# Products of probabilities with V issued in pairs of key tiles, in the attention of a one-core hybrid block

## What is computed

```python
q1, q2, k1, k2, v1, v2 = ...                     # 16 heads, D = 16, rotary on q and k
s = einsum('bthd,bshd->bhts', q, k) * scale      # causal mask
a = softmax(s)                                   # over the keys s
attn1 = concat(a1 @ v1, a1 @ v2); attn2 = concat(a2 @ v1, a2 @ v2)
attn = lowpass_over_tokens(attn1 - lambda_full * attn2)   # an FFT filter in the reference
attn = attn * rsqrt(mean(attn**2) + eps) * rms_weight * (1 - lambda_init)
x = x + attn.reshape(...) @ Wout
```

## Time and profile before

| | us |
|---|---|
| median of 3 runs | 1439.36 |
| lowest, highest | 1429.5, 1444.77 |
| the profiled execution | 1432.0 |
| its span in the trace | 1430.2 |
| TensorE busy in it | 1188.8 (83%) |
| VectorE, GpSimd, ScalarE busy | 892.3, 819.8, 602.6 |
| mean granted TensorE clock | 0.926 of full speed |

### The profile page before, as it was taken

One profiled execution on the slowest core, in us unless ns is written; L12 is line 12 of the kernel. 1 busy time (PEld: TensorE's weight loads), 2 busy tenths in 40 slices (PEclk: granted clock), 3 DMA queues, 4 the chain that ended last, 5 costly groups with the idle time before them and its releaser, 6 DMA issues. The chain is left out here.

```text
span 1430.2 us, 20085 instructions
## 1 busy us (share of the span) xinstructions
PE 1188.8 (83%) x7129; PEld 604.1 (42%) x7144; DVE 892.3 (62%) x1418; ACT 602.6 (42%) x969; POOL 819.8 (57%) x603
## 2 busy tenths in 40 slices
PE   5964888898898898898898888984679899986995
PEld 4721233333333433332332432422368777764443
DVE  5643756666666766665665775652666666663775
ACT  2310355565565555555555655662322232221121
POOL 4409457587687678678678674671025556663111
PEclk9987799899899999899999998986789999998997
DMA  4343220401401410410410310030422111113330
GB/s 146 114 135 97 74 77 12 118 23 38 118 30 31 119 40 21 119 43 18 119 42 18 104 56 5 1 133 0 166 87 74 59 64 70 45 45 103 125 103 38
DMA packets 72561, 101.20 MB, mean 71 GB/s; under 512 B 12432, under 2 KB 37904, under 8 KB 72464
## 3 DMA queue, kind: packets, MB, share of 16 engines
q1 hardware_dynamic: 61968, 70.57, 17.2%
q0 software_dynamic: 5888, 20.97, 3.8%
q10 hardware_dynamic: 4608, 8.39, 1.5%
HBM read 66.34 MB, written 33.55 MB: 70 GB/s over the span
## 5 line engine op out<-in xcount | busy, mean ns | idle before, releaser
L917 DVE TENSOR_REDUCE nm<-score 128x1 f32<-128x640 f32 (+6 forms) x352 | 348.8, 1024 | 275.6 <-PE score L802 210.3
L1127 POOL TENSOR_TENSOR base<-base,plain 128x2048 f32<-128x2048 f32 x48 | 218.7, 4556 | 79.0 <-ACT plain L1067 77.3
L1067 ACT ACTIVATE plain<-score 128x1024 f32<-128x1024 f32 (+3 forms) x288 | 208.1, 734 | 114.2 <-PE score L818 82.1
L813 PE MATMUL score<-qst,kst 98*128 98x512 bf16 (+7 forms) x768 | 201.2, 348 | 51.9 <-ACT plain L1067 28.2
L876 DVE TENSOR_TENSOR base<-base,plain 128x1536 f32<-128x1536 f32 (+2 forms) x96 | 165.1, 1720 | 15.5 <-ACT plain L1067 11.5
L712 PE MATMUL misc<-xnT,wg 128*128 128x512 f32 x256 | 128.6, 631 | 26.4 <-ACT raw L988 14.1
L1067 ACT ACTIVATE base<-score 128x1024 f32<-128x1024 f32 x96 | 98.1, 1024 | 86.8 <-PE score L818 45.8
L813 PEld LDWEIGHTS score<-qst,kst 98*128 98x128 bf16 (+1 forms) x768 | 57.1, 100 | 180.4 <-issue 67.7
L831 PE MATMUL acc<-plain,vg 128*32 128x512 f32 (+3 forms) x1152 | 116.8, 479 | 5.4 <-ACT plain L1067 4.9
L797 PE MATMUL score<-kst,qst 48*128 48x512 bf16 (+3 forms) x512 | 71.5, 358 | 46.7 <-DVE nm L917 26.9
L1431 PE MATMUL m_b<-m_winh,m_hTh 128*128 128x512 f32 x192 | 83.5, 435 | 13.9 <-DVE m_k L1610 12.5
(11 more groups left out here) (230 smaller groups left out, 2370.4 us busy)
## 6 DMA issues: line engine op xcount, KB each, us to landing
piece_scratch<-pieces POOLq DMA_DIRECT2D x16, 768.0 KB, 4.0
qst<-piece_scratch SPq DMA_DIRECT2D x192, 64.0 KB, 3.0
kst<-piece_scratch SPq DMA_DIRECT2D x192, 64.0 KB, 2.2
x1in<-in_query SPq DMA_DIRECT2D x16, 256.0 KB, 2.7
v_scratch<-v ACTq DMA_DIRECT2D x16, 256.0 KB, 2.0
vg<-v_scratch SPq DMA_DIRECT2D x8, 512.0 KB, 4.1
att_scratch<-y SPq DMA_DIRECT2D x8, 512.0 KB, 3.0
m_aT<-att_scratch SPq DMA_DIRECT2D x16, 256.0 KB, 2.9
```

Of the source, the lines that this page charges most:

```text
L813: mm = nc.tensor.matmul(score[k % RING][:, x, t0:HALF], kst[c, n % SLOTS, first + x, j * P:(j + 1) * P], qst[c, n % SLOTS, first + x, h * ...
L917: nc.vector.tensor_reduce(out, src, AX.X, ALU.max, negate=True).then_inc(s_max, 1)
L1067: nc.scalar.activation(tile_of(n, v)[:, first:first + 2, t0:HALF], score[k % RING][:, :, t0:HALF], ACT.Exp)\
L1127: nc.gpsimd.tensor_tensor(total, total, tile_of(n, v)[:, :, t0:HALF], ALU.add)\
```

## The change

The product of an even tile is no longer put behind its own probs steps, but directly ahead of the product of the odd tile that follows. Nothing else in the list moves.

```diff
@@ -408,6 +408,7 @@
 ROWS_OVER = 25
+PAIRED = 1
 ROOT_LATER, NEWTON_LATER = 3, 3
@@ -466,7 +467,11 @@
         for v in range(NV):
             k = at["probs", n, 2 * v + 1] + VALUES_LATER
-            put(k, ("values", n, v))
+            if not PAIRED:
+                put(k, ("values", n, v))
+            elif v % 2:
+                put(k, ("values", n, v - 1))
+                put(k, ("values", n, v))
             if v in ADDED:
                 put(k + ADD_LATER[ADDED[v][1]], ("add", n, v))
```

## The result

| | before | after |
|---|---|---|
| median, us | 1434.8 (4 runs, 1429.5 to 1444.77) | 1465.93 (4 runs, 1457.15 to 1466.34) |
| ratio | | 1.0215, interval 1.0177 to 1.0253 |
| profiled execution, us | 1432.0 | 1465.85 |
| its span, us | 1430.2 | 1464.0 |
| mean granted clock of TensorE in it | 0.926 | 0.912 |

The changed kernel is slower by 2.15%: 31 us between the medians, 34 between the two profiled executions. Forecast were 17 over 1439.4. The medians of before that came with the later runs (25, 28 and 7 of them) are 1433.75, 1432.79 and 1433.34. So the 1439.4 shown ahead was a few us high, and the 31 us are the better number.

What follows compares the result with a forecast made beforehand. TensorE, 83% busy, looked like the bound, with GpSimd nearly a second one in even sets (0.65 us to spare). Delays of +15.8 and clock +6 on 1432 gave 1454; forecast median 1456, 1.2% over 1439.4, range 1437 to 1468.

Steps and rivals of the forecast that it cites:

- The sum: Whole execution: +15.8 us of delays and +6 of clock over the profiled 1432, giving 1454; median forecast 1456.
- Add 5 waits for V4: GpSimd, even sets: add 5 overwrites tile 4, which the moved product V4 reads, so it starts 2.85 us late.
- Absorption by the gap before add 6: GpSimd, even sets: of 0.88 us idle before add 6, 0.7 absorbs delay; 2.15 us stays, making `shp` late.
- TensorE comes earlier to the turn, at 635.0: TensorE reaches its turning of `shp` 1.2 us earlier, then waits 2.8 us for GpSimd; the turn is 1.6 late.
- 2.5 us go through to each pair: Behind the turn of `shp`: 2.5 us late passes to the next pair of sets; five pairs, +12.5 us.
- the clock, "Seven new waits by 4/7 by 1.6 makes +6.4": New waits before the turn of `shp` lower TensorE's clock in some sets; bounds 0 and 11 us, +6 taken.
- n = 12 and 13, and n = 14 with the end: Late sets: +1.5 us for n = 12 and 13, +1.0 for n = 14, add 5 of the last set 1.3 late.
- the sets 0 and 1: First two sets, without a Newton step, keep some of the pairs' saving: -0.5 us.
- Only the drains count: Rival: TensorE is the bound and GpSimd isn't late; faster, median 1432 or so, 1425 with all drains; chance 0.09.
- No difference: Rival: short wait at the turn of `shp`, clock stays up; +6 to +12 us, 1445 to 1451; chance 0.29.
- Slower by more: Rival: each new wait lowers the clock and the odd set's long idle grows; +28 us, 1467; chance 0.12.
- About 13 us less of TensorE's busy time (in spite of the clock): Sign expected in the profile after: TensorE busy about 13 us less, with paired products 0.89 us apart.

Runs made afterwards that it cites:

- run 10: Kernel before with no product moved, only add 5 on GpSimd made to wait for V5 instead of V4; 1455.87 us, ratio 1.0147 to before.
- run 4: Changed kernel, all six pairs kept, with the second Newton step of a set six steps later, behind `shp`; 1436.04 us, ratio 1.0015 to before.
- run 2: Kernel before with only V4 and V5 (products with V of tiles 4 and 5) made a pair; 1464.22 us, ratio 1.018 to before.
- run 1: Changed kernel with V4 back at its old place and the other five pairs kept; 1440.09 us, ratio 1.006 to before.
- run 6: Changed kernel with V4 at its old place and the second Newton step of a set six steps later; 1445.47 us, ratio 1.0075 to before.
- run 8: Kernel before with pairs of the other parity, V1-V2, V5-V6 and V9-V10, the other products alone; 1447.28 us, ratio 1.0084 to before.
- run 3: Kernel before with only V0 and V1 made a pair; 1429.17 us, ratio 0.995 to before.

## Why the prediction was right, and where its sizes were off

Right in sign, in mechanism and within the range, too low by 14 of the 31 us. The sum itself was +22 on the profiled execution, where 33.9 were measured; the +17 of the median was a choice, over a median of before that was some 5 us high.

- **Add 5 waits for V4.** Forecast 2.85 late, measured 3.36: V4 began 13.56 us behind the anchor at 605.50 instead of 13.24, and add 5 1.24 us behind it instead of 1.05. The idle is ended by `acc` and no longer by ScalarE, as forecast. Run 10, in which add 5 waits for V5 at its old place, shows this one step to be worth 22 of the 31 us.
- **Absorption by the gap before add 6.** Forecast 0.7, leaving 2.15; measured 0.71 (0.88 - 0.17), and 2.64 left, the same half us too much as above.
- **TensorE comes earlier to the turn, at 635.0.** It didn't: 43.46 us behind the anchor instead of 43.51. The two products of a pair are 0.15 us cheaper each, near the forecast, but the -1.2 for V0's place and the pairs doesn't arrive at the turn. Between the anchor and the turn the rows have 2.05 us of idle time in six pieces, against 1.60 in three before, so small waits took up 0.45 of it; where the rest went isn't shown. So the wait was 2.19 instead of 2.8, and with it the turn was 2.14 late, not 1.6.
- **2.5 us go through to each pair.** Measured +2.6, +2.5 and +2.6 in n = 2, 6, 10, the three pairs without a fall of the clock behind the turn. The number is right, by two errors that cancel: the turn was 0.5 us later than forecast, and what was added behind it is 0.4 (2.5 less 2.14) instead of the 0.9 for V0.
- **The term that failed: the clock, "Seven new waits by 4/7 by 1.6 makes +6.4".** The count was right: it fell behind four of the seven. But the 4/7 was taken from other waits, and behind the turns of runs 2 and 10, with 1.5 and 1.8 us, it fell in none of n = 2 to 10, so that the count came out was luck. The price was wrong. It was taken from a fall of 3.4 us, seen from the next engine as 1.6 us. Measured are 6.8 us at 1.2 GHz behind the turn, and more later in the same pair: the pairs n = 4 and 8 cost 8.0 and 6.9, so 5.5 and 4.4 us above the 2.5. In the whole attention the time at 1.2 GHz went from 103 to 150 us. At half speed that is some 23 us of work's time; some of it lies in waits that were there anyway.
- **n = 12 and 13, and n = 14 with the end.** Forecast +1.5 and +2.3. Measured by the windows: 56.2 + 45.4 against 48.9 + 46.4 us, +6.3, and 74.2 against 69.0, +5.2. The turns of these sets waited 2.73 and 2.38 us (for n = 14 I had counted on 1.1 us of slack) and both brought the clock down. The windows of before, and V11 of the last set now, which starts at 1003.53 against 969.65:

```profile
805.30:854.20 48.90, 43.55 (x334) 18.40 (x336) 31.87 (x33) 28.44 (x40) 32.41 (x19) 0.97 0.18 54
854.20:900.60 46.40, 39.17 (x300) 13.92 (x300) 29.65 (x31) 25.71 (x35) 21.49 (x11) 0.89 0.06 16
900.60:969.60 69.00, 57.43 (x426) 22.15 (x428) 38.47 (x30) 43.26 (x61) 51.16 (x24) 0.92 0.19 69
...
1003.53 0.66 PE L836 MATMUL acc<-plain,vg 128*32 128x128 f32 x8 [4.91 <-ACT plain L1072]
```

- **The sum.** 15.8 for the delays was forecast, against the profiled execution. What came above it: 0.2 for the three quiet pairs together, 9.9 for n = 4 and 8, 4.8 for n = 12 and 13, 2.9 for the end, 0.2 for the sets 0 and 1 (-0.3 in place of -0.5). Together 33.8, and the profiled executions differ by 33.9. Of the 18.0 above, 9.9 is what sets with a fall behind the turn cost more than those without; the +6 stood for all of it.
- **Rivals.** "Only the drains count" falls: TensorE has fewer changes of division, and none of that reached the end. Even run 4, with all of them saved, 10 us less of TensorE's busy time in the attention and no wait at the turn, is no faster than before. By the rule in the Trainium skill's TensorEngine Tiling (Array Packing), Key Properties, changing the mode drains TensorE; the trace agrees for the single pair (0.93 us a product instead of 1.08). In run 4 the saving goes into waits for VectorE and ScalarE, 119.3 us instead of 108.5. "No difference" falls by the interval. "Slower by more" was the nearest in size, 1467 against 1465.93, at 0.12; but it needed a fall behind every wait and a longer wait in the odd set, and neither was so: three of seven passed without one.
- **"About 13 us less of TensorE's busy time (in spite of the clock)"** was wrong: it is 14 us more. The plain groups of products did fall, from 116.8 to 115.2 us, and the base groups rose from 54.9 to 58.1, since more of the lowered clock now lies over them. In run 4 it is there, 13.1 us less (1175.7 against 1188.8).

Left open: why runs 1, 6 and 8 lose 6 to 14 us with TensorE not waiting for `shp` up to n = 10, and why the kernels of runs 1 and 6 fall into two groups of times. It coincides with more time at 1.2 GHz (116, 152 and 129 us in the attention, against 103 before and 98 in run 4), but run 3 has 117 and isn't slower. It is not told by one wait's length, and no run here separates which wait lets the clock fall. Also open is where the half per cent of run 3 comes from.

## What to carry to other kernels

Before you move an instruction, ask who overwrites what it reads, on which engine, and what is queued in order behind that; an engine with 57% of busy time had less slack (0.65 us) than the move took. If a move is wanted all the same, look for something in the late engine's queue that isn't urgent and put it behind what is waited for: the Newton step six steps later gave back 30 us. And don't price a new idle time of TensorE by its own length alone: 1.5 us at each turn (run 2) made the pairs of sets 2 to 6 us longer, and falls of the clock of 3 to 10 us at half speed were part of that. Look too at every run's time and not only at a median, before two variants a few us apart are compared: runs 1 and 6 have two groups of times more than 8 us apart. The fastest version here leaves V4 alone and pairs V0 with V1, 1429.17 us (ratio 0.995, 0.9927 to 0.9973), though no trace shows what gave it the half per cent.

## What the runs showed of the hardware

- A wait of 2.19 us before the same instruction was followed by 6.8 us at 1.2 GHz in n = 8 and by none in n = 6 of the same execution. The length of the idle time alone doesn't tell it.
- Eight unread matmuls (1.67 us in the record of seven) in such a wait kept 2.4 GHz behind it in n = 4 and 8, and the five pairs of sets of that trace are 7 us shorter (545.9 against 552.9), though the matmuls shortened no chain. The medians agree (6.9 us) but aren't clear of the noise.
- One and the same kernel (run 6) ran five times at a mean granted clock of 0.923 to 0.932 in 1435.7 to 1441.2 us and five times at 0.914 in 1449.7 to 1451.6 us. In the trace of the upper group one pair of sets has 17 us at 1.2 GHz, and its pairs of sets all take about 109 us, so the falls repeat from pair to pair within an execution. But the order of the instructions alone doesn't fix them.
- More time at 1.2 GHz isn't by itself a longer kernel: run 3 has 117 us of it in the attention and before 103, and V11 of the last set begins at 970.18 and 969.65.
